# Tables and weights of a two-layer vision tower side by side in wide arrays, loaded from the SP and ACT queues

## The reference, cut to what matters

```
x (32, 3, 64, 64) -> 16 patches of 16x16x3 per image, times W.T + b; class token in front: h (32, 17, 128)
layer 0: xn = layernorm(h)
         retention, 8 heads of 16, complex weights:
           scores = (q k) * decay mask;  y = (scores v).real, normalised per head, * gn_scale + gn_bias
           h += (silu(xn @ w1.real) * yn) @ w2.real
         xn = layernorm(h); 2 shared + 8 routed experts (128 -> 512 -> 128, gelu), top 2 of 8; h += their sum
layer 1: xn = layernorm(h)
         attention, 8 heads of 64, scores mixed over the heads before (th1) and after (th2) the softmax; h += ...
         xn = layernorm(h); 32 experts (128 -> 128 -> 128, relu), top 2, each with a capacity; h += ...
out (32, 17, 128)
```

## Time and profile before

| | us |
|---|---|
| median of 3 runs | 222.42 (222.33 to 224.34) |
| the profiled execution's own time | 222.83 |
| its span, first to last instruction | 221.0 |
| PE busy in the span | 205.2 (93%) |
| DVE / ACT / POOL busy | 149.4 / 103.7 / 90.2 |

### The profile page before, as it was taken

How to read it: one execution, slowest core, us unless ns; L and a number is a source line. 1 busy time by engine, 2 the same in 40 slices (tenths; PEclk the granted TensorE clock), 3 DMA queues, 4 the chain that set the end, 5 groups by cost and what they waited for, 6 DMA issues and landing times.

```text
span 221.0 us, 4407 instructions
## 1 busy us (share of the span) xinstructions
PE 205.2 (93%) x1636; PEld 166.6 (75%) x1636; DVE 149.4 (68%) x425; ACT 103.7 (47%) x259; POOL 90.2 (41%) x110
## 2 busy tenths in 40 slices
PE   6999999797899999999998899989997999989984
PEld 2986676556799999999998566779986557866662
DVE  0353588587843578888899828576665799937684
ACT  2014842325957687778876373123353103633311
POOL 6126376861417774795891210000001610008740
PEclk9999999999799999999999999999999999999999
DMA  6899550000030764314000099000000000031111
GB/s 226 221 279 272 110 156 1 4 0 0 21 125 25 270 197 154 98 57 136 0 3 0 15 363 383 3 3 1 3 0 0 3 0 0 1 98 31 42 32 50
DMA packets 11119, 18.70 MB, mean 85 GB/s; under 512 B 3477, under 2 KB 5911, under 8 KB 10843
## 3 DMA queue, kind: packets, MB, share of 16 engines
q1 hardware_dynamic: 9994, 17.49, 24.5%
q0 software_dynamic: 1104, 0.94, 2.6%
HBM read 17.79 MB, written 0.82 MB: 84 GB/s over the span
## 4 chain that ended last, share of the span: by engine, by line
PE 72%; DVE 10%; DMA 5%; ACT 4%; SPq 4%; issue 3%; POOL 1%; DVEq 0%; ACTq 0%
PE ps L1806 69%; DMA w_slot<-in_w 5%; SPq L409 3%; PE ps L2232 2%; DVE acc L1364 1%; ACT ps L817 1%; SPq L414 1%; DVE hid_lo L1266 1%; ACT hid_hi L823 1%; DVE scaled L1361 1%; PE ps L1816 1%; DVE bn L1097 1%; DVE xn L1110 1%; DVE dots_m L1445 1%; DVE top_i L1505 1%
## 5 line engine op out<-in xcount | busy, mean ns | idle before, releaser
L537 POOL TENSOR_TENSOR ln_rstd<-ln_var,minus_half 119x1 f32<-119x1 f32 x20 | 11.0, 553 | 65.4 <-DVE ln_var L1105 65.3
L1266 DVE TENSOR_TENSOR hid_lo<-ps,hid_hi 128x544 fp32r<-128x544 f32 x36 | 24.8, 720 | 14.4 <-ACT hid_hi L823 14.2
L817 ACT ACTIVATE ps<-ps,b_cols 128x544 f32<-128x544 f32 x36 | 24.8, 690 | 12.6 <-PE ps L1806 11.7
L1806 PE MATMUL ps<-hid_hi,w_hi 128*128 128x272 f32 x80 | 23.7, 296 | 0.6 <-DVE hid_lo L1411 0.6
L1806 PE MATMUL ps<-hid_lo,w_hi 128*128 128x272 f32 x80 | 23.5, 293 | 0.0
L1806 PE MATMUL ps<-hid_hi,w_lo 128*128 128x272 f32 x80 | 23.5, 293 | 0.0
L1806 PE MATMUL ps<-filler 128*128 128x512 bf16 x79 | 21.7, 401 | 1.5 <-DVE filler L1170 1.5
L670 POOL DMA_INDIRECT rows_back<-o_spill,row_index x10 | 11.3, 1126 | 24.3 <-DMA o_spill<-o_rows 21.6
L823 ACT CAST hid_hi<-ps 128x544 fp32r<-128x544 f32 x36 | 20.8, 618 | 0.3
L1806 PE MATMUL ps<-xT_hi,w_hi 128*128 128x272 f32 x80 | 19.1, 313 | 1.9 <-DVE hid_lo L1266 1.9
L1806 PE MATMUL ps<-xT_lo,w_hi 128*128 128x272 f32 x80 | 17.5, 292 | 0.0
(11 more groups left out here) (240 smaller groups left out, 477.4 us busy)
## 6 DMA issues: line engine op xcount, KB each, us to landing
w_slot<-in_w SPq DMA_DIRECT2D x20, 256.0 KB, 3.6
m<-in_m SPq DMA_DIRECT2D x2, 2048.0 KB, 10.3
w_all<-w_spill SPq DMA_DIRECT2D x8, 272.0 KB, 4.0
patchesT<-in_patchesT SPq DMA_DIRECT2D x3, 357.0 KB, 8.1
w_qkv<-in_w_qkv SPq DMA_DIRECT2D x1, 768.0 KB, 13.7
front<-in_front SPq DMA_DIRECT2D x1, 741.0 KB, 4.4
o_spill<-o_rows SPq DMA_DIRECT2D x2, 256.0 KB
decay<-in_decay SPq DMA_DIRECT2D x1, 442.5 KB
```

Source lines behind the costliest of these rows:

```text
L537: nc.gpsimd.tensor_tensor(ln_rstd[:, g:g + 1], ln_var[:, g:g + 1], minus_half[:], ALU.pow).then_inc(rstd_ready, 1)
L817: nc.scalar.activation(chunk, chunk, ACT.Gelu, bias=b1_cols[:, e * FC + c:e * FC + c + 1]).then_inc(hid_ready, 1)
L1266: nc.vector.tensor_tensor(halves(hid_lo[:, e % 2, c, :]), ps[:, up_bank(e, c):up_bank(e, c) + 2, 0:HALF], halves(hid_hi[:, e % 2, c, :].bi ...
L1806: return nc.tensor.matmul(out_, lhsT, rhs, start=first, stop=last)
```

## The change

1. Arrays. The constants are laid side by side on the host in five arrays of 128 rows (`PACKS`): `front` (now with `embed_bias`; 1610 numbers a row, 805 KB of 1024 bytes), `early` (`ident`, `sign`, `gate_w`, `gate_b`, `iota`, `b1_cols`; 217 a row, 108.5 KB), `proj` (`w_proj`, `w_vg`; 1152, 576 KB), `ret` (`decay`, `centre_w`, `w_ret_out`, `gn_scale`, `gn_bias`; 1592, 796 KB), `late` (`w_qkv`, `w_out` and thirteen tables of layer 1; 3148, 1574 KB). Rows beyond a table's own are zero; broadcasts are written out on the host. First and second weights of an expert lie side by side too (1024 numbers a row, 512 KB an expert).
2. Queues. SP issues `front`, patches of groups 1 and 2 in one transfer (714 KB), `early`, patches of groups 3 and 4 in one (561 KB), `b2_rows`, `late`, `moe_b2`. ACT issues, ahead of everything else it does, `proj`, `ret`, and experts 0 and 1 (512 KB each). POOL issues nothing at the start; `before` and `pair_sel` move behind its `mixing_first(1)`, and `ones` goes (the ranks use the filler, which is all ones).
3. Order. Some instructions change places on every engine: on ACT `weights_high(0, 0)` now stands ahead of the third `turn_out`, on PE `scores(0)` behind `project_in(3, 1)`, `project_in(5, 1)` behind `scores(1)`, on POOL `mixing_second` and `mixing_first(0)` ahead of the last two `split_w2`; one filler matmul more at the start.

```
+PACKS = {
+    "front": (("patch_w", FRONT), ("patch0", KC * GT), ("embed_bias", D)),
+    "early": (("ident", 128), ("sign", 1), ("gate_w", ER), ("gate_b", ER), ("iota", EM), ("b1_cols", EA * FC)),
+    "proj": (("w_proj", 6 * 128), ("w_vg", 3 * D)),
+    "ret": (("decay", 8 * GT), ("centre_w", 2 * D), ("w_ret_out", D), ("gn_scale", D), ("gn_bias", D)),
+    "late": (("w_qkv", 3 * H * DH), ("w_out", 4 * D), ("b_v", H * DH), ("b_out", D), ("block", GT), ...
+}
+        def view(pack, name, p=128):
+            return pack[0:p, span(name)]
-            w1_slot = [sb_in(experts0, f"w1_slot{s}", [128, FF]) for s in range(2)]
-            w2_slot = [sb_in(experts0, f"w2_slot{s}", [128, FC, D]) for s in range(2)]
+            w_slot = [sb_in(experts0, f"w_slot{s}", [128, 2 * FF]) for s in range(2)]
# SP
             load("front", front[:], dram["front"])
-            for g in range(1, G):
-                own = slice(KC * (g - 1) * GT, KC * ((g - 1) * GT + rows(g)))
-                sp.dma_start(patchesT[:, own], dram["patchesT"][:, own]).then_inc(patches_loaded[g - 1], 16)
-                if g == 1:
-                    load("ident", ident[:], dram["ident"])
-            load("w_proj", w_proj[:], dram["w_proj"])
...
+            patches(0)
+            load("early", early[:], dram["early"])
+            patches(1)
             load("b2_rows", b2_rows[:], dram["b2_rows"])
+            load("late", late[:], dram["late"])
             load("moe_b2", moe_b2[:], dram["moe_b2"])
# POOL
-            load("embed_bias", embed_bias[:], dram["embed_bias"])
-            load("sign", sign[:], dram["sign"])
-            load("gn_scale", gn_scale[:], dram["gn_scale"].partition_broadcast(128))
-            load("gn_bias", gn_bias[:], dram["gn_bias"].partition_broadcast(GT))
...
             split_w2(7)
+            split_w1(9)
+            mixing_second()
+            mixing_first(0)
             split_w2(8)
-            split_w1(9)
             split_w2(9)
-            mixing_first(0)
-            mixing_second()
             mixing_first(1)
+            load("before", before[:], dram["before"])
+            load("pair_sel", pair_sel[:], dram["pair_sel"])
# ACT
+            def expert(e):
+                act.dma_start(w_slot[e][:], dram["w"][:, e, :]).then_inc(w1_loaded[e], 16)
+
+            load("proj", proj[:], dram["proj"])
+            load("ret", ret[:], dram["ret"])
+            expert(0)
+            expert(1)
             act.wait_ge(filler_ready, 1)
...
             turn_out(0, range(1, 2))
+            weights_high(0, 0)
             turn_out(0, range(2, 3))
             turn_out(0, range(3, 4))
             project_out(0, 0)
-            weights_high(0, 0)
# PE
-                    pe.wait_ge(patches_loaded[g - 1], 16)
+                    pe.wait_ge(patches_loaded[(g - 1) // 2], 16)
...
             project_in(0, 1)
-            scores(0)
             project_in(1, 1)
             project_in(2, 1)
             project_in(3, 1)
+            scores(0)
             project_in(4, 1)
-            project_in(5, 1)
             values_gates(1)
             scores(1)
+            project_in(5, 1)
```

More of the change, by code:

```diff
@@ L68 @@
 EPS = 1e-5
+PACKS = {
[3 more added lines that the diff above has]
+    "ret": (("decay", 8 * GT), ("centre_w", 2 * D), ("w_ret_out", D), ("gn_scale", D), ("gn_bias", D)),
+    "late": (("w_qkv", 3 * H * DH), ("w_out", 4 * D), ("b_v", H * DH), ("b_out", D), ("block", GT),
+             ("block_scaled", GT), ("th1", H * H), ("th2", 2 * H), ("sel_m", S), ("router_w", EM), ("moe_b1", EM),
+             ("b_qk", 8), ("slot_row", SLOTS), ("slot_col", 1), ("own_row", CHUNK)),
+}
+WIDTH = {pack: sum(n for _, n in parts) for pack, parts in PACKS.items()}
+PACK_OF = {name: pack for pack, parts in PACKS.items() for name, _ in parts}
 UP_BANKS = (2, 4, 0)
@@ L104, in rows, with span @@
     return min(GT, T - g * GT)
+def span(name):
+    parts = PACKS[PACK_OF[name]]
+    at = [n for n, _ in parts].index(name)
+    first = sum(w for _, w in parts[:at])
+    return slice(first, first + parts[at][1])
 def cols(g):
@@ L268, in build @@
         o_lo = sb("o_lo", [PAIR, QS - VIA, 4 * D], F32R)
[L271 to L278, removed]
+        alone = ("b2_rows", "moe_b2", "before", "pair_sel", "m1", "m2")
+        loaded = {n: sem("ld_" + n) for n in (*PACKS, *alone)}
         w1_loaded = [sem(f"w1_loaded{s}") for s in range(2)]
         w2_loaded = [sem(f"w2_loaded{s}") for s in range(2)]
-        patches_loaded = [sem(f"patches_loaded{g}") for g in range(1, G)]
+        patches_loaded = [sem(f"patches_loaded{k}") for k in range(2)]
         zeroed = sem("zeroed")
@@ L399, in here @@
             for n in names:
-                eng.wait_ge(loaded[n], 16 * max([1] + [len(names) for names in TOGETHER if n in names]))
+                eng.wait_ge(loaded[PACK_OF.get(n, n)], 16)
         def halves(ap):
@@ L541, in _ @@
             rstd(0)
-            load("pair_sel", pair_sel[:], dram["pair_sel"])
-            load("before", before[:], dram["before"])
-            load("ones", ones[:], dram["ones"])
             def split_w1(e):
@@ L561, in split_w2 @@
                 slot = e % 2
-                pool.wait_ge(w2_loaded[slot], 16 * (e // 2 + 1))
+                if e < NS:
+                    pool.wait_ge(w1_loaded[slot], 16)
+                else:
+                    pool.wait_ge(w2_loaded[slot], 16 * (e // 2))
                 if e >= 2:
@@ L1311, in _ @@
             head_var(4)
+            offset_heads(3)
             layer_stats(1)
@@ L2265, in rank @@
                 if k == 0:
-                    here(pe, "before", "ones")
+                    here(pe, "before")
                 for g in BATCHES[k]:
@@ L2649, in lay_out @@
     a["moe_b2"] = i["L1_ffn_b2"]
+    for pack, parts in PACKS.items():
+        wide = np.zeros((128, WIDTH[pack]), f)
+        for name, width in parts:
+            table = a.pop(name)
+            wide[:len(table), span(name)] = table.reshape(len(table), width)
+        a[pack] = wide
     return {k: np.ascontiguousarray(v) for k, v in a.items()}
```

182 lines of the change are left out of this document (86 added, 96 removed).

## The result

| | before | after |
|---|---|---|
| median, runs in turn with each other | 224.15 us (20 runs, 221.91 to 226.89) | 225.16 us (20 runs, 223.50 to 228.42) |
| profiled execution | 222.83 | 223.52 |
| its span | 221.0 | 221.7 |

The ratio after to before is 1.0071, with a 95% interval of 1.004 to 1.0103: some 0.7% slower, inside the 1% that I called no change. Executions more than 1.5% above the fastest of their own kernel are left out of all ratios; of the changed kernel's 20 these are four, at 228.3 to 228.4 us.

What follows compares the result with a forecast made beforehand. The start was taken as bound by PE fed with patches. Against 222.83, +2.6 - 0.6 - 0.3 - 0.7 = +1.0; set 0.4 over the 222.42 base median, it gave 223.4 us, range 219.6 to 226.2.

Steps and rivals of the forecast that it cites:

- part 1: Start: ACT's second queue is served beside SP's and delays the patches; embedding 3 starts at 15.2, not 12.59 us.
- Equal turns by array rows: Start: the two queues share DMA in equal numbers of array rows, one of `proj` for each of `front`; an estimate.
- Landings: Start: at 373 GB/s (bounds 330 to 400), `front` lands at 6.4 us, groups 1 and 2 10.5, 3 and 4 15.1.
- my two nearly equal bounds: Third embedding's start: PE's earlier work ends at 15.2 us, the last patches land at 15.1.
- +2.6 us of start: Embedding 3 and everything behind it come 2.6 us later because the patches land later.
- rival A: Start: SP's patches are not held up by ACT's queue; -1.8 us, time 220.6; chance 0.28.
- Late weights, -0.6: Expert 0 lands at about 12.2 us, not 19.8, ending PE's waits at xT and first scores; -0.3 to -0.8.
- Order, -0.3: Swapped instructions: second scores come one projection earlier, shortening DVE's stop after four decays; bounds -0.6 and +0.3.
- POOL's mixing products, -0.7: Line 1364 near 114 us: one mixing product left there frees DVE and PE; at the new place at most +0.3.
- The low stretch at 58 us: PE's half-clock stretch of 3 us, costing some 1.5 us, was assumed to stay.
- Rival B: Start: PE stays at its low clock level through groups 1 and 2; +1.9 us more, 225.3; chance 0.22.
- C: Whole kernel: moved loads have nobody waiting and reordering makes up late patches; 222.4 us, no change; chance 0.08.

Runs made afterwards that it cites:

- act_after_front: The changed kernel, but ACT issues its four loads only when `front` has landed; 223.50 us (10 runs), ratio 0.9907.
- one_queue: The changed kernel, but all loads from SP, in order of use (`proj`, `ret`, experts 0 and 1 behind the patches); 222.88 us (6 runs), ratio 0.9836.
- packs_old_order: The changed kernel's arrays and ACT loads, with the order of work on all engines as in the kernel before; 225.97 us (6 runs), ratio 1.0022.
- after_again: The changed kernel once more, no edit, in a later session; 226.02 us (12 runs) against 226.76 for the kernel before, ratio 0.9998.
- mix_early: The changed kernel with POOL's three mixing products moved behind `split_w1(2)`; 225.79 us (14 runs), ratio 0.9972.
- pool_order_before: The changed kernel with POOL's last splits and mixing products in the order of the kernel before; 228.22 us (4 runs, too wide to use as a time).
- after_more_fillers: The changed kernel with twelve filler matmuls for eight ahead of the first embedding and four behind it; 226.56 us (12 runs), ratio 1.0002.
- before_again: The kernel before, no edit, profiled twice more; 224.94 and 226.84 us, one execution each.

## Why the prediction was right, and where by luck

The number was 223.4 and the profiled execution took 223.52, but the median of 20 is 225.16. Against the kernel before in the same runs the change costs 1.0 us by the medians and 1.6 by the ratio (0.0071 x 224.15), where I had +1.0. The mechanism of part 1 held: ACT's queue is served beside SP's and holds up the patches. The page DMA: Bandwidth & Descriptors of the Trainium skill (Issuing engines are not separate DMA queues) says that the transfers of all issuing engines interleave on the same 16 engines; the landings in pairs agree, with 4.2 us as the price. Equal turns by array rows, for which I had no row, fit these landings. By the turns between queues that the prediction took from the same page (Queues, rings and completion order), act_after_front should have shown later patches than it did; they landed as in one_queue.

- **Landings.** `front` 6.4 forecast, 6.75 measured; groups 1 and 2 10.5 and 10.5; groups 3 and 4 15.1 and 14.8; projections near 19.0 and 18.60. The rate was 419 to 444 GB/s in the windows shown and not 373, above my upper bound of 400. It did not show much, since `front` had less idle time to fill than I allowed. PE, too, was forecast to reach the third embedding only at 15.2, with 3.97 us for groups 1 and 2; it took 2.88 and then waited 0.85 us for the last patches. Only the landing bounded the start, which my two nearly equal bounds had left open.
- **+2.6 us of start.** Measured +2.2, from two large terms that I had not taken apart: +4.2 for the queue (one_queue to after), -2.0 from before to one_queue, for the arrays and PE's level together. "I use 373 GB/s for all of it" hid that the arrays in one queue would put the patches at 6.9 and 8.7 us, and rival A's "PE needs until 12.4 for three groups anyway" took PE's low level for PE's pace. Against the other two executions of before the start costs -0.2 and -0.8, not +2.2: the step took one execution's 8.1 us for the kernel's own.
- **Late weights, -0.6.** Right for the execution I read, 0.62 by U-P (35.78 to 35.16), and nothing where the patches come later. The two costs cover each other, so a sum that takes both from one execution has both right and neither in general.
- **Order, -0.3.** Measured 35.16 to 34.89, so -0.27, or -0.1 by packs_old_order. None of the swaps moved PE by 1 us.
- **POOL's mixing products, -0.7.** This step failed: +0.65. I had put the bound at +0.3 on the ground that DVE has 0.92 us of idle time before `split_w2(8)`. The 0.92 us stands before `hid_lo` at 104.14, but the products begin at 105.45, when DVE is at work again and has none to give. The change also puts `split_w1(9)` ahead of `split_w2(8)`; it stands at 102.99 to 105.5 and uses up POOL's idle time, which I had given to the products. They run straight into `w_hi`, and the addition waits for three POOL instructions instead of two. The half of the step that looked at the old place held, 0.53 us of the 0.7; the new place cost 1.15 where I had at most 0.3. POOL's loads cost nothing: beside them, at 115.63, the addition takes 0.44.
- **The low stretch at 58 us.** I left it where it is; it went in this execution, -1.4, and is back in after_again. Without it the sum to A would be 2.22 - 0.62 - 0.27 + 0.62 = +1.95, with it +0.51.
- **Rival B** holds too, in other executions. In after_again, mix_early and pool_order_before the embeddings of groups 1 and 2 took 5.47 us (4.73 in packs_old_order), in after 2.88, and but for packs_old_order with the same wait before them: three of the six profiled executions of this start, and in part a fourth. I had given it 0.22. Four of the changed kernel's 20 executions took 228.3 to 228.4 us, as the traced after_again did (228.40); that they start like it is likely and not shown, since no trace of them is kept. I had forecast 5.8 and a cost of 1.9; P is 1.86 to 2.0 later. The condition I gave (embeddings more than 1 us after the first ends) was not it: the gap was 0.80 us in both. The Trainium skill (TensorE: Matmul & The Clock Gate, Part 1) has idle PE falling to half clock; in the one traced execution of after_more_fillers PE kept its full level over a wait of 1.28 us behind a busy stretch, and in after_again it had the low one behind 0.80; so one wait's length, on which I had hung it, doesn't tell.
- **Rivals A and C** fell: A by the landings, C by the milestones. The later session's 0.9998 is C's time and not shown to be C's cause: of the late start the new order made up 0.27 us.

The total of the profiled execution came out near the forecast because the terms that were off (the missing gain of the mixing products, 1.3 us; the lost low stretch, 1.4) cancelled: luck. The ratio went from 1.007 to 0.9998 between sessions; the kernel before stood at 224.2 and 226.8 us in them, and the one whose patches land irregularly is the kernel before. That its P is later in the second session's executions is inferred from three profiles and not shown for the medians. The sessions also ran on different chips, and that is not separated from it. On the one chip of the two before_again executions the landings still differed (9.3 and 9.9 us), and a third execution there, without a trace, took 223.71 us.

## What to carry to other kernels

Wide arrays gained only where the order in which bytes are needed was kept: the second queue that started with the first took about half of the bandwidth for what it carried. Let it start when the last urgent transfer is close to done, and don't put a cast that waits for its data ahead of copies that PE needs. Before a start is costed from one profile, take two or three more profiles of the same kernel; read two equal bounds of a start apart, since a wait that shows as zero can hide one; and place POOL products where POOL is idle and DVE does not add.

## What the runs showed of the hardware that was not expected

- DMA held 419, 428 and 444 GB/s in the three windows shown of 3 to 17 us with arrays of 128 rows, and 319 where four small tables from POOL were among them.
- DVE's addition of two SBUF operands, 0.44 us when undisturbed, took 2.62 us beside three POOL instructions in a row (two mixing products and `w_hi`). They follow one another with no gap (106.11 to 106.06, 107.20 to 107.15); the first gap, 108.20 to 108.28, stands 0.3 us before DVE ends. The Trainium skill (SBUF — State Buffer, SBUF: two separate sides) gives the shared ports to one instruction at a time, and these rows show a wait of more than one instruction. That DVE gets no turn where there is no gap would fit them, but not others: the addition at 113.24 ends 0.3 us after a `w_lo` whose successor had begun without a gap, and that successor took 1.32 us where the same product took 1.14 at 106.06. So DVE got its turn behind `w_lo` and none behind a mixing product; why stays open.

```profile
113.24 1.31 DVE L1364 TENSOR_TENSOR acc<-acc,scaled 128x272 f32<-128x272 f32 x1
```

```profile
112.97 1.28 POOL L558 TENSOR_TENSOR w_lo<-w_slot,w_hi 128x512 fp32r<-128x512 f32 x1
114.21 1.32 POOL L609 TENSOR_TENSOR mix_w<-late 119x544 f32<-119x544 f32 x1
```

- The granted clock read 1.00 from 10 to 16 us in after_again while 24 matmuls took 5.47 us, which took 2.88 in after; packs_old_order, with 4.73 us, showed 0.63 in the same stretch. In these starts the duration of equal matmuls told the level, and the granted clock did not always.
- All profiled executions but the one of after hold stretches at half the granted clock, up to four, at places that change (7 to 15, 45 to 49, 58 to 66, 198 to 224 us). Most lose 1.4 to 1.7 us; the longest, in one_queue from 207 to 218, loses 5. They are of the size of the scatter, 2 to 5 us. What brings the late ones stays open.
